# Two tiles of roots, multiply-then-add on GpSimd and dense identity products in a twelve-layer perceiver kernel

## The reference

```python
def _layernorm(x, axis=-1, eps=1e-05):
    m = jnp.mean(x, axis=axis, keepdims=True)
    v = jnp.var(x, axis=axis, keepdims=True)
    return (x - m) / jnp.sqrt(v + eps)
...
    def _l2_normalize(t):
        n = jnp.sqrt(jnp.sum(t * t, axis=-1, keepdims=True))
        return t / jnp.maximum(n, EPS)
```

## Time and profile before

| | |
|---|---|
| median of 3 runs | 3743.85 us (3743.23 to 3745.98) |
| the profiled execution | 3772.4 us |
| its span | 3770.2 us |
| busy share PE, DVE, ACT, POOL | 79%, 66%, 54%, 52% |
| mean granted clock of TensorE | 0.884 of full |

### The profile page before, as it was taken

One profiled execution on the slowest core, in us unless ns is written; L12 is line 12 of the kernel. 1 busy time (PEld: TensorE's weight loads), 2 busy tenths in 40 slices (PEclk: granted clock), 3 DMA queues, 4 the chain that ended last, 5 costly groups with the idle time before them and its releaser, 6 DMA issues. The chain is left out here.

```text
span 3770.2 us, 79125 instructions
## 1 busy us (share of the span) xinstructions
PE 2981.6 (79%) x23619; PEld 2060.2 (55%) x23619; DVE 2481.5 (66%) x6661; ACT 2041.2 (54%) x6345; POOL 1973.8 (52%) x1964
## 2 busy tenths in 40 slices
PE   6989596779999697575999996787862668968967
PEld 5769434446666585453677773333322436735645
DVE  7966676658888573333788885898985123447863
ACT  5545405658888454223677774555530125549954
POOL 5630205767777793053566664888870541117830
PEclk9989798989999798788899998998985778968979
DMA  3300001322222000111111112444431229800000
GB/s 102 91 26 0 6 1 60 101 68 81 79 80 76 8 1 6 59 37 42 41 36 36 36 35 103 135 141 135 146 107 60 31 41 232 199 7 1 2 7 22
DMA packets 142430, 233.64 MB, mean 62 GB/s; under 512 B 28796, under 2 KB 104862, under 8 KB 141575
## 3 DMA queue, kind: packets, MB, share of 16 engines
q1 hardware_dynamic: 134088, 221.61, 20.1%
q0 software_dynamic: 8128, 9.45, 1.4%
HBM read 200.44 MB, written 13.71 MB: 57 GB/s over the span
## 5 line engine op out<-in xcount | busy, mean ns | idle before, releaser
L3208 PE MATMUL l2a_pY<-l2a_hc,ident 128*128 128x512 f32 x512 | 273.4, 673 | 91.3 <-POOL l2a_hc L3127 56.9
L2446 POOL TENSOR_TENSOR l2x_att_prob<-l2x_att_prob,l2x_att_rs 128x1024 f32<-128x1024 f32 x128 | 242.5, 1895 | 148.3 <-DVE l2x_att_rs L2677 148.3
L3097 POOL TENSOR_TENSOR l2a_dbu<-l2a_dx,l2a_BC 128x1024 f32<-128x1024 f32 x128 | 298.7, 2355 | 20.8 <-PE l2a_pY L3208 10.6
L2446 POOL TENSOR_TENSOR l1x_att_prob<-l1x_att_prob,l1x_att_rs 128x1024 f32<-128x1024 f32 x128 | 242.6, 1895 | 106.9 <-DVE l1x_att_rs L2677 106.9
L2634 ACT ACTIVATE l2x_att_prob<-l2x_att_pS,l2x_att_nmx 128x257 f32<-128x257 f32 x512 | 236.4, 475 | 94.5 <-DVE l2x_att_nmx L2672 94.5
L3225 ACT ACTIVATE l2a_pA<-l2a_dl,l2a_A 128x512 f32<-128x512 f32 x256 | 174.7, 690 | 187.7 <-DVE l2a_pH L3331 112.5
L2634 ACT ACTIVATE l1x_att_prob<-l1x_att_pS,l1x_att_nmx 128x257 f32<-128x257 f32 x512 | 236.4, 475 | 72.9 <-DVE l1x_att_nmx L2672 72.8
L3208 PEld LDWEIGHTS l2a_pY<-l2a_hc,ident 128*128 128x128 f32 x512 | 103.6, 211 | 252.8 <-issue 119.4
L2672 DVE TENSOR_REDUCE l1x_att_nmx<-l1x_att_pS 128x1 f32<-128x257 f32 x512 | 182.0, 418 | 89.2 <-PE l1x_att_pS L2545 89.2
L3331 DVE TENSOR_TENSOR_SCAN l2a_pH<-l2a_pA,l2a_dbu 128x512 f32<-128x512 f32 x192 | 224.9, 1217 | 23.5 <-POOL l2a_dbu L3097 12.3
L2672 DVE TENSOR_REDUCE l2x_att_nmx<-l2x_att_pS 128x1 f32<-128x257 f32 x512 | 182.0, 418 | 53.4 <-PE l2x_att_pS L2550 53.4
(11 more groups left out here) (741 smaller groups left out, 9086.4 us busy)
## 6 DMA issues: line engine op xcount, KB each, us to landing
l2a_BC<-l2a_rows SPq DMA_DIRECT2D x128, 512.0 KB, 3.8
l3x_att_ctn<-ctx_n SPq DMA_DIRECT2D x32, 576.0 KB, 12.4
l0x_att_kvs<-ctx_t SPq DMA_DIRECT2D x32, 514.0 KB, 3.6
l1x_k_xin<-ctx_t SPq DMA_DIRECT2D x32, 514.0 KB, 3.5
l1x_att_ctx<-ctx_t SPq DMA_DIRECT2D x128, 128.5 KB, 2.1
l1x_att_kT<-l1x_KA SPq DMA_DIRECT2D x128, 128.5 KB, 2.2
l2x_att_ctx<-ctx_t SPq DMA_DIRECT2D x128, 128.5 KB, 2.1
l3x_att_ctx<-ctx_t SPq DMA_DIRECT2D x32, 514.0 KB, 10.7
```

What stands on the lines that cost most here:

```text
L2446: pool.tensor_tensor(p, p, bc(rs[:, b, :], 2, LAST), ALU.mult).then_inc(scaled, 1)
L3097: pool.tensor_tensor(dbu[:, u % 3], dx[:, g % 2], bc(BC[:, u % RING, 0, :], 1, NC), ALU.mult).then_inc(dbu_made, 1)
L3208: last = pe.matmul(pY[c][:, :], env.ident[:, :], hc[:, u % 3, c, :], start=False, stop=n == NS - 1)
```

## The change

Four things are changed. `head_projection` has two tiles of roots, and `roots(n)` waits for the factors of n - 2. In mode "ln" DVE's multiplication loses the gain, and POOL's instruction becomes multiply by the gain, then add the shift. In `normalise` POOL's tiles become multiply by `rstd`, then add `shifted`, and POOL takes tiles 3, 6 and 7 of a chunk, ACT 4 and 5. For the residual's norm of `l1a_ln1` DVE makes `shifted1` with one more small instruction for each chunk. Last, `busy` multiplies the identity by itself, 512 columns at a time, into a bank that is not yet used: seven times at the start of PE's program in every transposing norm but `l0x_ln` (twelve stages), and six times in layer 0's `route` ahead of the wait for the weights.

```diff
+def busy(pe, env, bank, times):
+
+    for _ in range(times):
+        pe.matmul(bank[:, :].rearrange("p (r d) -> p r d", r=4), env.ident[:, :], bc(env.ident[:, :], 1, 4))
+
...
-                            last = pool.tensor_scalar(dst[:, t, :], src[:, t, :], mv[:, t, 0:1], once[:, t:t + 1],
-                                                      ALU.subtract, ALU.mult)
+                            last = pool.tensor_scalar(dst[:, t, :], src[:, t, :], once[:, t:t + 1],
+                                                      shifted1[:, t:t + 1], ALU.mult, ALU.add)
...
-                        for t in (c * PER + split - 1, c * PER + PER - 1):
-                            pool.tensor_scalar(main[:, t, :], src[:, t, :], mv[:, t, 0:1], rstd[:, t:t + 1],
-                                               ALU.subtract, ALU.mult).then_inc(by_pool, 1)
+                        for share in ((split - 1,), (PER - 2, PER - 1)):
+                            for t in share:
+                                last = pool.tensor_scalar(main[:, c * PER + t, :], src[:, c * PER + t, :],
+                                                          rstd[:, c * PER + t:c * PER + t + 1],
+                                                          shifted[:, c * PER + t:c * PER + t + 1], ALU.mult, ALU.add)
+                            last.then_inc(by_pool, 1)
...
+                    if both:
+                        dve.scalar_tensor_tensor(out=shifted1[:, r], in0=mv[:, r, 0], scalar=-1.0, in1=once[:, r],
+                                                 op0=ALU.mult, op1=ALU.mult)
...
-                    for t in list(tiles(c))[split:PER - three]:
+                    for t in list(tiles(c))[split:PER - 2 * three]:
...
+                if constants is None:
+                    busy(pe, env, pst[0], 7)
...
+                if WT is not None:
+                    busy(pe, env, pw[0], 6)
                 pe.wait_ge(w_ready, 1)
...
-        sd = st.sb("sd", [P, wide])
+        sd = st.sb("sd", [P, 2, wide])
...
                             pool.tensor_scalar(parts[i].dst[:, piece(n, u)], y[:, n % 3, u, 0:width(n)],
-                                               cols[i][:, 0:1], None, ALU.add).then_inc(done, 1)
+                                               cols[i][:, 1:2], cols[i][:, 0:1], ALU.mult, ALU.add).then_inc(done, 1)
...
                     past(act, var_made, n)
-                    past(act, r_made, 4 * (n - 1) + 3)
+                    past(act, r_made, 4 * (n - 2) + 3)
...
                         if ln:
-                            dve.scalar_tensor_tensor(out=yu, in0=yu, scalar=cols[i][:, 1:2], in1=ru, op0=ALU.mult,
-                                                     op1=ALU.mult).then_inc(r_used, 1)
+                            dve.tensor_tensor(yu, yu, ru, ALU.mult).then_inc(r_used, 1)
```

More of the change, by code:

```diff
@@ L120, in normalise @@
         if both:
-            std1, once = st.sb("std1", [P, TILES]), st.sb("once", [P, TILES])
+            std1, once, shifted1 = st.sb("std1", [P, TILES]), st.sb("once", [P, TILES]), st.sb("shifted1", [P, TILES])
         if dst_t is not None or onto is not None:
@@ L2265, in factors @@
                         past(pe, r_used, 4 * n + u - 3)
-                        pe.matmul(pR[(4 * n + u) % 3][:, 0:width(n)], spread[r, :], sd[r, 0:width(n)]
+                        pe.matmul(pR[(4 * n + u) % 3][:, 0:width(n)], spread[r, :], sd[r, n % 2, 0:width(n)]
                                   ).then_inc(r_made, 1)
@@ L2308, in roots @@
                     past(act, var_made, n)
-                    past(act, r_made, 4 * (n - 1) + 3)
+                    past(act, r_made, 4 * (n - 2) + 3)
                     m = width(n)
                     if ln:
-                        act.activation(sd[:, 0:m], pV[:, 0:m], ACT.Sqrt, bias=env.eps[:, 0:1]).then_inc(sd_made, 1)
+                        act.activation(sd[:, n % 2, 0:m], pV[:, 0:m], ACT.Sqrt, bias=env.eps[:, 0:1]).then_inc(sd_made, 1)
                     else:
-                        act.activation(sd[:, 0:m], pV[:, 0:m], ACT.Sqrt).then_inc(sd_made, 1)
+                        act.activation(sd[:, n % 2, 0:m], pV[:, 0:m], ACT.Sqrt).then_inc(sd_made, 1)
                 projected(0)
@@ L2334, in _ @@
                     if not ln:
-                        dve.tensor_scalar(sd[:, 0:m], sd[:, 0:m], 1e-12, None, ALU.max).then_inc(sd_step, 1)
+                        dve.tensor_scalar(sd[:, n % 2, 0:m], sd[:, n % 2, 0:m], 1e-12, None, ALU.max).then_inc(sd_step, 1)
                         past(dve, sd_step, n)
-                    dve.reciprocal(sd[:, 0:m], sd[:, 0:m]).then_inc(rs_made, 1)
+                    dve.reciprocal(sd[:, n % 2, 0:m], sd[:, n % 2, 0:m]).then_inc(rs_made, 1)
                     for u in range(4):
```

## The result

The changed kernel took 3709.84 us (median of four runs, 3707.17 to 3725.38) beside 3743.54 us for the kernel before on the same chip (four runs, 3739.39 to 3745.98). The ratio is 0.9922, with a 95% interval from 0.9896 to 0.9947, so about 29 us less (20 to 39); the medians themselves lie 33.7 us apart. 28.5 were forecast. That the totals agree this well is partly luck, as the stages will show. The profiled execution of the kernel after took 3725.38 us, the longest of its four runs.

The account below looks back on a forecast made before the run. No single engine was taken to bound the kernel; stages have limits of their own. 0 + 1 + 10 + 11 + 0 + 7.5 - 1 = 28.5 us off 3743.85 gave about 3715 us, range 3692 to 3762.

Parts of the forecast that it names:

- Step 1: Head projection, two tiles of roots: 0 us, bounds no loss and at most 28 us gained.
- the root was in the loop: Rival: an earlier root shortens each head projection unit by up to 0.63 us, 20 to 28 us more; chance 0.06.
- Step 2: Head projection, gain moved to POOL: 0.94 us an instruction stays hidden, about 1 us gained in the tail.
- The dear rival: Multiply-then-add on POOL costs what subtract-multiply does: 20 to 55 us slower, 3764 to 3799; chance 0.18.
- Step 3: POOL's norm tiles as multiply-then-add: 0.5 us for 128 columns, 10 us saved in `l1a_ln1` (0 to 11.5).
- the pair is in between: Rival: POOL's pair takes 0.6 to 0.75 us for 128 columns, under 1.25 for 257; 3728 to 3740; chance 0.12.
- Step 4: POOL takes three of eight norm tiles: 1.2 us in each of nine norms without router, 11 us.
- Step 5: Identity products in norms: 0 in nine plain norms, 2.5 us each in three with a router, 7.5 together (1 to 18).
- Step 6: Identity products in the route: 1 us lost, bounds 5 gained to 3 lost.
- identity products don't pay: Rival: clock falls again in norms' gaps, cold products delay first groups; about 3729 us (3723 to 3733); chance 0.12.
- The clock of the head projections: Moves by itself: eight `l3a_q` units could gain up to 14 us, or some `l1x_k` units lose as much.

Follow-up runs that it names:

- e5: Kernel after with POOL's pair in the first head projection as subtract, then multiply (another result there); 3713.34 us, ratio to before 0.9922.
- e7: Kernel after with POOL's norm tiles as subtract-multiply again, still three of eight; 3765.34 us, ratio to before 1.0069.
- e6: Kernel before with multiply-then-add for POOL's norm tiles, still two of eight; 3736.73 us, ratio to before 0.9986.
- e8: Kernel after with two of ACT's eight copies given to DVE in norms without a router; 3706.99 us, ratio to before 0.9908.
- e4: Kernel after without any identity products; 3715.63 us, ratio to before 0.9933.
- e9: Kernel after once more, unchanged, on the third group's chip; 3724.65 us, ratio to before 0.9895.
- e2: Kernel before with the identity products alone, in twelve norms and the route; 3734.25 us, ratio to before 0.9973.
- e10: Kernel after with two copies on DVE and identity products only ahead of layer 0's and 1's routers; 3724.32 us, ratio to before 0.9887.
- e11: Kernel after with two copies on DVE and no identity products at all; 3727.38 us, ratio to before 0.99.
- e1: Kernel before, unchanged, run and profiled once more; 3743.28 us, ratio to before 0.9991.
- e3: Kernel before with two tiles of roots and the looser wait alone; 3740.97 us, ratio to before 1.0001.

## Why the prediction was right, and where it was not

*Step 1, two tiles of roots: right.* 0 forecast, a ratio of 1.0001 measured alone, and the loop of 4.99 us unchanged in the profile. The rival "the root was in the loop" is excluded: 20 to 28 us would have been a ratio of 0.9925 to 0.9947, outside 0.9981 to 1.0021. The profile does name the factors as what the root waits for; that was true and cost nothing: PE is through with all but the last of the factors that the root feeds, and then idle for 0.59 us until ACT's squares let it start the variances.

*Step 2, the gain on POOL: right in its effect, wrong in its price.* I took 0.94 us, the row of the single add; it is 0.563. The tail came as forecast: from DVE's last multiplication to the next stage 5.3 us before and 4.1 after, 1.3 gained where 1 was taken. The dear rival's price here was wrong too, and in a way that mattered for its chance: I scaled from 128 columns with 0.2 us fixed and got 1.42, where 1.237 was measured, below the 1.25 from which POOL would bind. So the 19 to 40 us that the rival put into `l1x_k` would not have come even with the dear pair (`e5` has 2.5 us more in the tail and the same unit). The loss of `e7` is in the norms and in the logits behind them.

*Step 3, POOL's tiles: right.* 0.5 us taken, 0.463 to 0.489 measured, which also excludes the rival "the pair is in between" (0.6 to 0.75). `l1a_ln1` lost 11.6 us (35.4 before, 23.7 after), at the cap, where 10 was forecast. The Trainium skill, "GPSIMD Engine Reference", section "Elementwise — side-by-side cycle accounting", has bodies of up to two operations bound by the port. Multiply-then-add fits it in so far as two operations cost no more than one (0.563 us against 0.942 for the single add, 257 columns); subtract-then-multiply on the same shape doesn't (1.237 us), and the rule doesn't tell the two apart.

*Step 4, three of eight: right.* 1.2 us forecast for each plain norm, 1.1 measured: 17.43, 17.63 and 17.48 became 16.32, 16.51 and 16.37 (before and after in their first profiles), hence about 10 us for the nine instead of 11, and the last copy of `l2x_ln` ends 15.55 us behind the start, where 15.5 was forecast. `e6`, with the cheap pair and two of eight, leaves them unchanged, and `e8` shortens them again by taking work from ACT. `e7` shows the other side: 0.2 to 1.7 us lost each, where 0.7 to 2.3 was worked out.

*Step 5, identity products in norms: the step that failed.* 0 in the plain norms was right (16.51 with, 16.47 without, in `l2x_ln`), and the time of the products, 6.25 to 9.20 us, is near the 7.7 to 9.5 that I took. For the three norms with a router I took 2.5 us each. The kernel after and `e4` beside each other: layer 0's norm and logits 23.6 against 29.0 us, layer 1's logits 13.9 against 16.9, layer 2's 17.05 against 10.8. That is 5.4 and 3.0 gained and 6.2 lost, 2 us together instead of 7.5.

In `e5`, `e8` and `e9`, with the same products and POOL's cheap pair in three tiles, layer 0's norm and logits took 22.8 to 23.5 us and layer 1's logits 11.1 to 11.6, which makes 5 us together; with the dear pair (`e7`) layer 0 gained nothing (29.2). So the term is 2 to 5 us, against kernels without products whose own stages vary (see `e2`), and what failed is its distribution: one mean of 2.5 us for three stages of which two gained and one lost 6.

That the clock can fall again in the norm's gaps stood in my list only as a rival, and it is what the windows of layer 2 show. Layer 2 was the one with something to lose: it starts near full clock (0.92 in its first window in `e4`, where layers 0 and 1 have 0.50), and its logits were mostly at full clock already, which also speaks against step 5's "logits of 8 columns let the clock fall again" as a rule. Those rows stood in my list, and I read them only as a price.

The 17.05 us came in each of the five profiles that have these products in this norm together with three of eight (after, `e5`, `e7`, `e8`, `e9`), and not in `e2`, which has the products and two of eight (11.1 us). So it takes both: a warm start, and POOL's share, which moves the pieces. The fall itself is in `e2` as well; what is missing with three of eight is the rise behind it. Why was not isolated.

*Step 6, the route: within its bounds.* 1 us lost was forecast; the route takes 14.0 us with the products and 13.9 without (after and `e4`), and 13.8 to 14.8 over all profiles, with products and without: nothing. Behind it, the experts of layer 0 took 96.0 in the kernel after and in `e2`, and 92.0 to 92.2 in `e5`, `e7`, `e8` and `e9`, all with the products; 92.2 in `e10`, with the router norm's alone; 90.4 and 90.6 in `e4` and `e11`, without any. That speaks for a small loss of some 2 us, but in four profiles without the products and with two of eight (before, `e1`, `e3`, `e6`) it took 96.1, 92.1, 96.1 and 92.0, so I leave it open.

*The sum, by what was measured.* Gained: 0 (roots), 1.3 (tail), 11.6, 10, 2 to 5 and 0 (route), and two terms that I hadn't named, both in stages that the change doesn't touch and in every kernel with the faster norms: `l3x_q` takes 22.4 us instead of 24.1, its first four instructions 1.96 us (after) instead of 3.04 (`e1_before_again`), and the experts of layer 2 (`l2f_exp`) 129.7 to 130.6 instead of 132.5 to 132.8, the first eight instructions of their first layer 5.44 us instead of 6.46. So the clock rises earlier there; why, and what the rest of the second term is, stays open. That is 1.7 and 2.4 more, and makes 29 to 32 us, where 29 (between 20 and 39) were timed; without the products it makes 27, where `e4` gave 25. Other stages differ by 1 to 2 us in either direction, so the sum is no closer than that. My 28.5 came near because the unnamed terms and step 3 made up for step 5. That is luck in the total, with the larger steps right.

*The rival "identity products don't pay"* (3729, a gain of 15) is half right: in the kernel as changed they are worth 2 to 5 us by the stages and can't be seen in the timing of `e4` against after. It failed in its sum because the other parts give 25 without them. The clock of the head projections moved by itself, as I had said: `l3a_q` took between 50.6 and 61.7 us over the profiles, with the same code, a unit taking 5.06 us at full clock and 6.7 otherwise. It went both ways, and is one part of the scatter of 20 us and more between single runs of a kernel.

## What to carry to other kernels

Before a wait is removed, add up the loop without it: here 0.74 + 2.91 + 0.14 + 0.57 + 0.63 was the whole period, and a named wait of 1.5 us was worth nothing. Where an engine's pair of operations can be written in two ways, measure both: on GpSimd the choice decided between 29 us gained and 26 lost. And before adding warm-up products on TensorE, read which clock the stage has without them: here they gained where it started at the low level and lost 6 us where it started high and rose again by itself. Last, a profile is one execution: the same stage of the same kernel took 10.7 us and 16.9, so the worth of a change needs several profiles, or a part measured alone.

## What the runs showed of the hardware

- GpSimd's tensor_scalar depends on which operations it does and not on how many: at 257 columns multiply-then-add 563 ns, one add 942 ns, subtract-then-multiply 1237 ns; at 128 columns 463 ns for multiply-then-add and 807 ns for subtract-then-multiply. Whether the order or the subtraction makes it dear was not tested.
- In layer 2 of the kernel after, TensorE stayed at a granted clock of 0.50 in windows of transposes and logits that have it busy 4.00 us of 4.00, 40 logits taking 8.54 us. Without the identity products the same work went from 0.80 to 1.00.
- Each warm-up of 14 instructions took a time of its own, between 6.25 us, all at full clock, and 9.20. A short idle time ahead of it didn't settle which: in the kernel after, layer 2's router norm (1.93 us idle) and `l3f_ln` (1.70) have 6.25, but `l1a_ln1` (1.72) 8.90 and `l1a_ln2` (1.46) 8.95.
- The chosen experts of layer 1 took 131 to 133 us in nine profiles and 150 to 153 in four, with the same code and nothing between. All three profiles on the third group's chip are of the slower kind, and one elsewhere, the first of before. What it is was not looked into.
